# A three-layer graph network on one core: the shift of every unit is added by VectorE instead of mostly by GpSimd

## The reference, cut to what matters

```python
residual = 0.0
for Wl, bl, Wr, g, b in params:              # 3 layers, Wl and Wr are 512 x 512
    msg = h[src]
    agg = segment_sum(msg, dst) / maximum(count(dst), 1)
    h = residual + agg @ Wl.T + bl + h @ Wr.T
    mu, var = mean(h), mean((h - mu) ** 2)   # over the 512 features of a node
    h = (h - mu) * rsqrt(var + EPS) * g + b  # g is the gain, b the shift
    h = where(h >= 0, h, a_prelu * h)
    residual = h
out = layernorm(x + h)
```

## Time and profile before

| what | value |
|---|---|
| median of three runs | 2066.18 us |
| the profiled execution | 2066.36 us, its span 2064.5 us |
| mean granted TensorE clock | 0.986 |
| TensorE busy | 1987.2 us, 96% |
| VectorE busy | 1551.7 us, 75% |
| ScalarE busy | 1208.0 us, 59% |
| GpSimd busy | 1444.0 us, 70% |
| GpSimd's shifts, 207 | 539.8 us, 2608 ns each |

### The profile page before, as it was taken

How to read it: one execution, slowest core, us unless ns; L and a number is a source line. 1 busy time by engine, 2 the same in 40 slices (tenths; PEclk the granted TensorE clock), 3 DMA queues, 4 the chain that set the end, 5 groups by cost and what they waited for, 6 DMA issues and landing times. The chain is left out here.

```text
span 2064.5 us, 30403 instructions
## 1 busy us (share of the span) xinstructions
PE 1987.2 (96%) x10149; PEld 1651.7 (80%) x10149; DVE 1551.7 (75%) x2412; ACT 1208.0 (59%) x2643; POOL 1444.0 (70%) x1092
## 2 busy tenths in 40 slices
PE   6899999999999999999999999999999999999992
PEld 4778888788888888888888888887788888888882
DVE  7668677667566655666666666669999999999994
ACT  3775545445444455544444444458877777777774
POOL 2566888888888776655555555546778888888886
PEclk8999999999999999999999999999999999999996
DMA  5568666576666555544444444456666666666552
GB/s 184 180 214 272 194 218 223 187 226 201 206 214 207 181 160 175 166 153 153 153 152 147 150 148 148 143 169 200 221 222 209 209 209 214 204 210 209 202 186 89
DMA packets 181073, 387.66 MB, mean 188 GB/s; under 512 B 20117, under 2 KB 20562, under 8 KB 180918
## 3 DMA queue, kind: packets, MB, share of 16 engines
q1 hardware_dynamic: 142358, 272.06, 39.8%
q0 software_dynamic: 38560, 113.67, 17.6%
HBM read 221.07 MB, written 164.79 MB: 187 GB/s over the span
## 5 line engine op out<-in xcount | busy, mean ns | idle before, releaser
L402 PE MATMUL ps_z<-w_hi,hT_hi 128*128 128x512 f32 x1884 | 763.2, 405 | 8.0 <-ACT ps_z L528 7.3
L402 PE MATMUL ps_z<-w_hi,hT_lo 128*128 128x512 f32 x1884 | 738.8, 392 | 0.0
L402 PE MATMUL ps_z<-w_lo,hT_hi 128*128 128x512 f32 x1884 | 738.4, 392 | 0.0
L673 POOL TENSOR_TENSOR y<-y,shift 128x1024 f32<-128x1024 f32 x207 | 539.8, 2608 | 166.6 <-DVE y L778 164.4
L528 ACT COPY ps_z<-bias_rows 128x512 f32<-128x512 f32 x471 | 276.4, 587 | 439.0 <-DVE y L778 390.2
L766 DVE TENSOR_TENSOR hT_lo<-ps_t,hT_hi 128x1024 fp32r<-128x1024 f32 (+1 forms) x237 | 287.3, 1212 | 325.8 <-ACT hT_hi L499 325.1
L402 PEld LDWEIGHTS ps_z<-w_hi,hT_hi 128*128 128x128 f32 x1884 | 354.7, 188 | 79.3 <-issue 12.4
L508 ACT ACTIVATE junk<-ps_z 128x512 f32<-128x512 f32 x471 | 277.9, 591 | 239.0 <-PE ps_z L402 230.8
L402 PEld LDWEIGHTS ps_z<-w_hi,hT_lo 128*128 128x128 f32 x1884 | 353.8, 188 | 79.1
L402 PEld LDWEIGHTS ps_z<-w_lo,hT_hi 128*128 128x128 f32 x1884 | 355.0, 188 | 67.1
L659 POOL TENSOR_TENSOR rstd<-veps,minus_half 128x2 f32<-128x2 f32 (+1 forms) x240 | 238.5, 994 | 228.8 <-ACT veps L518 228.6
(11 more groups left out here) (132 smaller groups left out, 2011.9 us busy)
## 6 DMA issues: line engine op xcount, KB each, us to landing
h_scratch<-hout SPq DMA_DIRECT2D x156, 512.0 KB
hin<-h_scratch SPq DMA_DIRECT2D x156, 512.0 KB, 3.8
x_by_slot<-hin SPq DMA_DIRECT2D x78, 512.0 KB
o_sb<-x_by_slot SPq DMA_DIRECT2D x78, 512.0 KB
rowtab<-edge_row_table SPq DMA_DIRECT2D x60, 256.0 KB
stage<-in_WrT SPq DMA_DIRECT2D x3, 1024.0 KB
stage<-in_WlT SPq DMA_DIRECT2D x3, 1024.0 KB
hin<-in_x,node_get POOLq DMA_INDIRECT x157
```

The source lines that it names most:

```text
L402: mm = pe.matmul(acc, a[:, k, :], ww[:, k, :], start=False, skip_group_check=True, stop=stop and k == KC - 1 and a is a_lo)
L673: nc.gpsimd.tensor_tensor(y[u.r2][:, 0:u.n, :], y[u.r2][:, 0:u.n, :], moved, ALU.add).then_inc(shifted, 1)
```

## The change

All 237 shifts become VectorE's, each in one instruction right behind the unit's `normal`. `here` and its counts go, GpSimd's `add_shift` and its call go, and one semaphore is left of two. Nothing else moves.

```diff
-    def here(no):
-        l, pos = divmod(no, UL)
-        return pos < LEAD and (l == 0 or l == L - 1 and pos % 2 == 0)
...
-            self.here = here(no)
-            self.shifts = len([n for n in range(no + 1) if here(n) == self.here])
...
-            def add_shift(u):                      # GpSimd
-                if u.here:
-                    return
-                if u.shifts == 1:
-                    pool.wait_ge(affine_signed, 1)
-                pool.wait_ge(gained, u.upto)
-                moved = shift[:, u.l:u.l + 1, :].to_broadcast([P, u.n, D])
-                nc.gpsimd.tensor_tensor(y[u.r2][:, 0:u.n, :], y[u.r2][:, 0:u.n, :], moved, ALU.add).then_inc(shifted, 1)
...
-                if last.exists:
-                    add_shift(last)                # GpSimd, end of its step
...
-            def add_shift_here(u):                 # VectorE
-                if not u.here:
-                    return
+            def add_shift(u):
                 dve.wait_ge(gained, u.upto)
                 moved = shift[:, u.l:u.l + 1, :].to_broadcast([P, u.n, D])
-                nc.vector.tensor_tensor(y[u.r2][:, 0:u.n, :], y[u.r2][:, 0:u.n, :], moved, ALU.add).then_inc(shifted_here, 1)
+                nc.vector.tensor_tensor(y[u.r2][:, 0:u.n, :], y[u.r2][:, 0:u.n, :], moved, ALU.add).then_inc(shifted, 1)
...
             def prelu(u):
-                dve.wait_ge(shifted_here if u.here else shifted, u.shifts)
+                dve.wait_ge(shifted, u.no + 1)
...
                     normal(last)
-                    add_shift_here(last)
+                    add_shift(last)
```

More of the change, by code:

```diff
@@ L250, in build_program @@
         squared, veps_done, rstd_done = sem("squared"), sem("veps_done"), sem("rstd_done")
-        gained, shifted, shifted_here, h_done, affine_signed = (
-            sem("gained"), sem("shifted"), sem("shifted_here"), sem("h_done"), sem("affine_signed"))
+        gained, shifted, h_done, affine_signed = sem("gained"), sem("shifted"), sem("h_done"), sem("affine_signed")
         rt_in = sem("rt_in")
@@ L686, in gpsimd_program @@
             for T in range(-3, UNITS + 6):
-                last = Unit(T - 1)
                 if 0 < T < UNITS + 4:
```

## The result

The changed kernel takes 2045.59 us in the median of five runs (2043.44 to 2046.63), the kernel before 2066.49 (2065.83 to 2066.69): a ratio of 0.9899 with a 95% interval of 0.9888 to 0.9909, so 1.0% faster. The profiled execution took 2046.63 us with a span of 2044.8, against 2064.5. In the changed program L393 is the matmul, L490 `take_high`, L509 `variance`, L519 `fill`, L552 `out_norm`, L639 the gather of messages, L650 `root`, L662 `put_out`, L682 the DMA that was L701, L729 `split_weight`, L757 `normal`, L778 the add, L784 `prelu` and L826 `out_sum`.

A forecast was written before the change was run, and what follows sets the result against it. It took TensorE to bound layer 1, VectorE (98% busy) the last edge part, three nearly level engines the last lead. Gains 8 + 4 + 3 + 3.2 = 18.2 us took 2066.4 to 2048.2, median 2048.0 us; range 2040 to 2060.

The forecast's parts named there:

- VectorE's adds: VectorE, all layers: 207 more adds at 1.14 us, 236 us of work; in the last edge part 94.5 us of stalls go.
- Layer 0: First 12 triples: the gap behind a stretched `split_weight`, its half clock and half the small gaps go; 8 us, at most 9.8.
- The lead of the last layer: `root` no longer sits behind GpSimd's add; a step falls from 7.4 to 7.1 us, 4 us, bounds nothing to 7.
- The last edge part: Last layer: VectorE drops below TensorE, 23.2 against 26.3 us a triple; gain 3 us, between 1 and 5.
- The end: Behind TensorE's last product: `root` no longer held by GpSimd's adds, 1.9 and 1.3 us; gain 3.2, bounds 2 and 4.
- GpSimd's queue: GpSimd: 7.2 us a triple freed, 3.1 lost to DMA instructions held by VectorE's adds; no row later, counted as nothing.
- the stretched add: Rival, last edge part: each VectorE add stretched to 3.0 us like `out_sum`, 44 us more there, about 2099 us; chance 0.04.
- shut out for a whole add: Rival, last lead: VectorE's add holds `root`, a step takes 8.1 us instead of 7.4; 2063 us, chance 0.08.
- The third rival: Another gap and clock dip replace layer 0's, the lead stays at 7.4 us a step; 2060 us, chance 0.18.
- TensorE's pace in the lead: Rival: everything goes to TensorE's pace, the last lead at 6.4 us a step; 34 us in all, 2032 us, chance 0.05.

The follow-up runs named there:

- experiment 3: The changed kernel plus a GpSimd addition of the same size, into an unread tile, at its old adds' places in layers 1 and 2: 2148.78 us.
- 4: The changed kernel plus a write-only GpSimd fill of 2048 columns of an unread tile at its old adds' places in layers 1 and 2: 2046.40 us.
- experiment 1: The kernel before, with the adds of all of layer 0 on VectorE, layers 1 and 2 as they were: 2057.12 us.
- experiment 2: The kernel before, with only those layer 0 adds moved to VectorE that fall near the steps that split weights: 2057.63 us.
- experiment 9: The kernel before, with the ten adds GpSimd had left in the last layer's lead moved to VectorE, edge parts as before: 2060.50 us.
- experiment 10: The changed kernel plus two write-only GpSimd fills, 2048 and 512 columns, at its old adds' places in layers 1 and 2: 2050.14 us.
- experiment 7: The changed kernel, with VectorE's `out_mean` right behind `out_sum` and one ScalarE `out_square` moved ahead of `out_norm`: 2036.56 us.
- experiment 11: The changed kernel run once more, unaltered, for a second profile: 2046.21 us.
- experiment 5: The kernel before, with the adds of layers 0 and 2 on VectorE and those of layer 1 left on GpSimd: 2044.97 us.

## Why the prediction was right, by its steps

It said 2048.0 us, in a range from 2040 to 2060, with 0.90 for faster. 2045.6 came out, 20.9 us below the kernel before where 18.2 were forecast.

- **VectorE's adds** cost 1225 ns in the median as read from the earlier trace rows, and the 94.5 us of stalls counted from the earlier trace rows are gone; the edge part is TensorE's again. VectorE was to be 88% busy there and is 89%. That a GpSimd instruction that reads SBUF stretches VectorE's two-input instructions, and a write of 1.83 us at the same place does not, is shown by experiments 3 and 4 together.
- **Layer 0** was forecast at 8 and gave 9.7 in the profile, 9.5 in the runs of experiment 1. The chain that the step named (stretched `split_weight`, late `carry`, gap, half clock) is confirmed by experiment 2, which moves the adds of those steps alone. I had counted half of the small gaps; all of them went.
- **The lead of the last layer** was forecast at 4. Its steps 4 to 18 went from 103.3 to 99.7 us, and experiment 9 puts the whole at 5.5; the wait of ScalarE was 0.8 us a step for the 0.7 forecast. But the term's gain rested on one reason, the place of `root` behind the add, and that explains only 0.6 of the 3.6 us, as far as a write of 2.4 us at that place can tell (experiment 10). So the size came out near the forecast by luck. The rest came only with an instruction that reads, so I put it down to the stalls; by which way they reach ScalarE's wait was not tried by itself. And the 7.1 us step that I worked out is in fact two in turn, 6.97 and 7.23. That ScalarE's wait sets the step is shown by experiment 7.
- **The last edge part** was forecast at 3, between 1 and 5. From the last layer's first cast to TensorE's last product it is 665.0 us before, 659.7 in experiment 9 and 656.1 in experiment 11, where the clock does not fall. That is 5.3 for the lead and what follows from it, and 3.6 for the edge part.
- **The end** was forecast at 3.2 and gave 3.2, from 36.2 to 33.0 us; here the place in the queue was the cause (experiment 10).
- **GpSimd's queue** was counted at nothing. That was wrong by 1.4 to 3.6 us in the last layer (its steps 18 to 77 take 511.4 us in the profile of experiment 5, without the gap, 512.8 in that of 11 and 515.0 in that of the changed kernel): DMA instructions held by VectorE, one by the add as the earlier trace rows showed and the next by `prelu`, go with late first messages of the last layer, a gap of 1.5 to 2.1 us and at times a half clock. The price was right (1.0 us each), and the cover that I named, GpSimd's slack of the whole layer, is not there in that step: it runs `root`, two `put_out` and two gathers in a row while TensorE comes near.

That the sum came within 3 us is in part a matter of cancelling: layer 0 and the lead gave 1.5 us more each than forecast and the edge part some 0.6, and the late messages took 1.4 to 3.6 back.

Of the rivals, the stretched add exists: it is the one add of 2.56 us beside `add_diagonal`, and experiment 3 shows what many such collisions do, 30.0 us a triple and 4% slower than the kernel before. The kernel has just no other long reader on GpSimd left. `root` was not shut out for a whole add. The third rival came true in a small part: another gap with a clock dip did come up, but in the last layer and not in layer 0, and the lead did not stay at 7.4 us a step. TensorE's pace in the lead was out of reach by this change, and experiment 7, with another order, comes near it.

## What to carry to other kernels

When two engines get in each other's way, the cost of an instruction is also what it does to its neighbour's: here 1.2 us on VectorE took the place of 2.6 us on GpSimd and of up to 2.3 us of VectorE's own time. Look for instructions of one shape with two durations, and at what runs beside the long ones. Work put on an engine that is 98% busy can relieve it, if that share is stalls. And when an engine waits for a chain of small steps, as ScalarE here for `root` and `omove`, moving an independent instruction into the wait can be worth as much as any move between engines.

## What the runs showed of the hardware

A write-only GpSimd instruction (a fill of 2048 columns, 1.83 us) does not stretch VectorE's two-input instructions, while an addition (2.41 us in the earlier trace rows, 3.48 in experiment 3) stretches them by 2.3 and 1.2 us in the lines shown. Instructions of VectorE that read PSUM are not stretched: in the kernel before no `normal` takes over 0.75 us and no `take_low` over 1.23. The reverse holds too: when VectorE's add starts 0.05 to 0.09 us ahead of an indirect DMA's instruction on GpSimd, that takes 1.95 to 2.04 us in both profiles of the changed kernel (2.48 in one case each) instead of 0.95 to 1.0, and beside a `prelu` the message DMA took 1.98. When the DMA instruction starts first, or up to 0.04 us behind the add's start, it takes 0.94 to 1.06. A gap of TensorE of 2.1 us was followed by 3.4 us at 1.2 GHz in one profile, and one of 1.5 us at the same place by none in another. The gap of 3.3 us in layer 0 is still there in experiment 9, but the clock behind it is at the low level for about 3.4 us there and for about 6.8 in the kernel before, and layer 0 is only 0.3 us shorter. Two windows of experiment 9, columns as in the earlier trace rows:

```profile
388.20:391.50 3.30, 3.30 (x8) 2.59 (x9) 3.30 (x6) 0.88 (x2) 2.59 (x3) 0.54 0.68 233
391.70:395.00 3.30, 3.30 (x16) 2.66 (x15) 2.28 (x4) 2.05 (x6) 2.67 (x4) 0.98 0.77 181
```
